# Gated adapter with layer norm on one core: the last batch's hidden stage made whole instead of by halves of its tokens

## The reference

```python
Wd = W_down[stream]; bd = b_down[stream]; Wu = W_up[stream]; bu = b_up[stream]
g = ln_w[stream]; b = ln_b[stream]
h = jnp.einsum('bsh,bhk->bsk', hidden_states, Wd) + bd[:, None, :]
h = jax.nn.gelu(h, approximate=False)
h = jnp.einsum('bsk,bkh->bsh', h, Wu) + bu[:, None, :]
h = hidden_states + h
mean = jnp.mean(h, axis=-1, keepdims=True)
var = jnp.mean(jnp.square(h - mean), axis=-1, keepdims=True)
h = (h - mean) * jax.lax.rsqrt(var + LN_EPS)
return h * g[:, None, :] + b[:, None, :]
```

## Time and profile before

| what | value |
|---|---|
| time, median of 3 runs | 72.03 us (71.99 to 72.11) |
| the profiled execution's own time | 72.03 us |
| its span, first to last instruction | 69.9 us |
| PE (TensorE matmul) busy | 57.6 us, 82% |
| DVE (VectorE) busy | 50.0 us, 72% |
| POOL (GpSimd) busy | 39.8 us, 57% |
| ACT (ScalarE) busy | 34.9 us, 50% |
| mean granted TensorE clock | 0.951 |

### The profile page before, as it was taken

One profiled execution on the slowest core, in us unless ns is written; L12 is line 12 of the kernel. 1 busy time (PEld: TensorE's weight loads), 2 busy tenths in 40 slices (PEclk: granted clock), 3 DMA queues, 4 the chain that ended last, 5 costly groups with the idle time before them and its releaser, 6 DMA issues. The chain is left out here.

```text
span 69.9 us, 947 instructions
## 1 busy us (share of the span) xinstructions
PE 57.6 (82%) x290; PEld 46.6 (67%) x290; DVE 50.0 (72%) x95; ACT 34.9 (50%) x51; POOL 39.8 (57%) x43
## 2 busy tenths in 40 slices
PE   1980199999499999999999999999999999994000
PEld 1960144489188888888887888888899989881000
DVE  0057005699929969883799989549999989999930
ACT  3300196898999800649998071999016504030000
POOL 4000060095199908999996599999929603038400
PEclk9999856999999999999999999999999999999955
DMA  0806999999999999999500006430000157210352
GB/s 0 265 35 161 344 246 401 416 414 413 415 412 414 413 411 417 397 413 415 206 16 0 0 5 260 197 143 0 0 9 0 61 239 300 86 65 5 148 203 100
DMA packets 4324, 14.75 MB, mean 211 GB/s; under 512 B 480, under 2 KB 480, under 8 KB 4320
## 3 DMA queue, kind: packets, MB, share of 16 engines
q1 hardware_dynamic: 4176, 14.17, 52.6%
q10 hardware_dynamic: 144, 0.52, 2.3%
HBM read 10.50 MB, written 4.19 MB: 210 GB/s over the span
## 5 line engine op out<-in xcount | busy, mean ns | idle before, releaser
L353 DVE BATCH_NORM_STATS2 stats<-y_ps 128x6 f32<-128x512 f32 x16 | 11.1, 694 | 4.2 <-PE y_ps L528 4.2
L522 PE MATMUL y_ps<-wu_hi,hid_hi 128*128 128x512 f32 x32 | 13.6, 424 | 0.0
L528 PE MATMUL y_ps<-wu_hi,hid_lo 128*128 128x512 f32 x32 | 12.8, 399 | 1.0 <-DVE hid_lo L342 1.0
L223 POOL TENSOR_TENSOR rstd<-var_eps,minus_half 128x2 f32<-128x2 f32 (+1 forms) x10 | 6.4, 641 | 12.2 <-DVE var_eps L361 12.2
L207 POOL TENSOR_TENSOR x_lo<-x_raw,x_hi 128x512 fp32r<-128x512 f32 x10 | 12.8, 1304 | 0.0
L524 PE MATMUL y_ps<-wu_lo,hid_hi 128*128 128x512 f32 x32 | 12.6, 393 | 0.0
L218 POOL TENSOR_TENSOR wu_lo<-w_raw,wu_hi 128x512 fp32r<-128x512 f32 x8 | 10.4, 1318 | 3.3 <-ACT wu_hi L274 3.3
L370 DVE SCALAR_TENSOR_TENSOR y_ps<-y_ps,mean_var,ln_gb 128x512 f32<-128x512 f32 x16 | 11.5, 749 | 0.0
L380 DVE SCALAR_TENSOR_TENSOR result<-y_ps,rstd,ln_gb 128x512 f32<-128x512 f32 x15 | 10.8, 744 | 0.3
L282 ACT ACTIVATE x_res<-x_raw,w_raw 128x512 f32<-128x512 f32 x16 | 10.3, 717 | 0.8 <-DMA x_raw<-x_cols 0.8
L334 DVE CAST x_hi<-x_raw 128x512 fp32r<-128x512 f32 x6 | 3.6, 596 | 9.5 <-DMA x_raw<-x_cols 9.5
(11 more groups left out here) (35 smaller groups left out, 84.9 us busy)
## 6 DMA issues: line engine op xcount, KB each, us to landing
x_raw<-x_cols SPq DMA_DIRECT2D x7, 512.0 KB, 11.5
out<-result SPq DMA_DIRECT2D x6, 512.0 KB, 2.6
w_raw<-weights SPq DMA_DIRECT2D x4, 516.0 KB, 10.9
w_raw<-weights SPq DMA_DIRECT2D x4, 512.0 KB, 11.6
ln_gb<-ln_rows SPq DMA_DIRECT2D x4, 512.0 KB, 14.8
out<-result SPq DMA_DIRECT2D x4, 256.0 KB, 2.4
x_raw<-x_cols ACTq DMA_DIRECT2D x1, 512.0 KB, 3.6
```

The lines of the kernel that those rows point to most:

```text
L353: nc.vector.bn_stats(stats[:, b % 2, t, :], y_ps[:, t, :]).then_inc(stats_done, 1)
L522: nc.tensor.matmul(y_ps[:, t, :], hid_hi[:, p, j, rows], wu_hi[:, p, j, :], start=False, stop=False, skip_group_check=True)
L528: last = nc.tensor.matmul(y_ps[:, t, :], hid_lo[:, p, j, rows], wu_hi[:, p, j, :], start=False, stop=(j == JT - 1), skip_group_check=True)
```

## The change

The last batch's down stage, gelu, subtraction and up stage are done as in the other batches. All helpers for halves go. The core of the diff:

```diff
@@ scalar @@
-                    gelu(b, 0)
-                    gelu(b, 1)
+                gelu(b, 0)
+                gelu(b, 1)
+                if b < LAST:
                     hi_x(b + 1, 1)
-            for half in range(2):
-                for j in range(JT):
-                    gelu_half(half, j)
@@ vector @@
-                if b + 1 < LAST:
-                    finish(b, 0)
-                    finish(b, 1)
-                    lo_hidden(b + 1, 0)
-                    finish(b, 2)
-                    finish(b, 3)
-                    lo_hidden(b + 1, 1)
-                else:
-                    finish(b, 0)
-                    lo_hidden_half(0, 0)
-                    finish(b, 1)
-                    lo_hidden_half(0, 1)
-                    finish(b, 2)
-                    lo_hidden_half(1, 0)
-                    finish(b, 3)
+                finish(b, 0)
+                finish(b, 1)
+                lo_hidden(b + 1, 0)
+                finish(b, 2)
+                finish(b, 3)
+                lo_hidden(b + 1, 1)
...
-                if t == 0:
-                    lo_hidden_half(1, 1)
@@ tensor: up @@
-                if b == LAST and t >= 2:
-                    n += JT
-                if t == 0 or (t == 2 and b == LAST):
+                if t == 0:
@@ tensor @@
-            for b in range(LAST):
+            for b in range(B):
...
-            down_half(0, 0)
-            down_half(0, 1)
-            down_half(1, 0)
-            place_residual(LAST, 0)
-            place_residual(LAST, 1)
-            up(LAST, 0, 0)
-            up(LAST, 0, 1)
-            down_half(1, 1)
-            up(LAST, 1, 0)
-            up(LAST, 1, 1)
-            for t in range(2, TT):
-                place_residual(LAST, t)
-                for j in range(JT):
-                    up(LAST, t, j)
```

More of the change, by code:

```diff
@@ L136, in conditional_adapter_kernel @@
         EARLY = KT + HALF
[L138 to L142, removed]
         SHARED_T = 1
@@ L291, in gelu @@
                                      bias=bias_down(b, j)).then_inc(hid_done, 1)
[L293 to L299, removed]
             act.dma_start(x_raw[:, 0, 0:HALF, :], x_cols[0, :, 0:HALF, :]).then_inc(x_in[0][0], DMA)
@@ L343, in lo_hidden @@
                                         ALU.subtract).then_inc(hid_lo_done, 1)
[L345 to L349, removed]
             def tile_stats(b, t):
@@ L480, in down @@
                 last.then_inc(hid_ps_done, 1)
[L482 to L500, removed]
             def place_residual(b, t):
```

## The result

The changed kernel took 73.3 us in the median of 4 runs (72.96 to 73.56), the kernel before 72.01 (71.98 to 72.11): ratio 1.0174, 95% interval 1.013 to 1.0218. It is slower by 1.3 us; the forecast was 73.44 with a range of 73.15 to 73.8. The profiled execution is the slowest of the four, 73.56 us with a span of 71.4. Three single runs further on (72.86 us of the kernel before, 73.94 and 72.93 of two of the experiments) lie over 1.5% above the fastest run of their kernel, and the ratios leave them out.

A forecast was written before the change was run, and what follows sets the result against it. The prediction took tile 0's arrival at VectorE plus a fixed VectorE chain as the bound. Its terms, 1.15 + 0.69 - 0.33 - 0.10 = +1.41 us on 72.03, gave 73.44 us, range 73.15 to 73.8.

The forecast's parts named there:

- What bounds the kernel: End of the last batch: the moment tile 0 reaches VectorE plus a fixed VectorE chain of 9.77 us before the change.
- Down stage, +1.15: TensorE, last batch: all the down stage precedes the residuals, 5.47 us instead of 4.32, so they begin 1.15 us later.
- Order of the up stage, +0.69: TensorE, last batch: tile 1's first group comes between tile 0's two groups, 2.72 us instead of 2.03, 0.69 us more.
- Gelu and subtraction hidden: Last batch: second half's hid_lo is ready at 58.08, wanted by the ninth product at 58.64, 0.56 us to spare.
- The chain, -0.33 and -0.10: VectorE after tile 0 arrives: fourth half subtraction (0.33 us) and wait for tile 2 (0.10) go, 9.77 becomes 9.34 us.
- The sum: VectorE's end in the last batch: 1.15 + 0.69 - 0.33 - 0.10 = +1.41 us, 68.42 against 67.01.
- The prediction's bounds: Whole time: 73.2 to 73.8 us from down stage, 0.10 wait, last store and 0.12 us run spread; widened to 73.15 below.
- the prediction's signs of being wrong: Last batch: tile 0's statistics before 58.8, a TensorE wait for hid_lo, or a chain under 9.2 or over 9.6 us.
- Saturated VectorE: Rival: VectorE's total work sets the end, so fewer, larger instructions save 0.53 us, time 71.50; chance 0.02.
- No change: Rival: the later delivery is taken up between tile 0 and the end, 1.41 us of slack, time about 72.0; chance 0.02.
- the third rival: Tail: tile 3's small variance instruction meets GpSimd work, or hid_lo comes over 0.56 us late; 0.53 us more, 73.97; chance 0.07.

The follow-up runs named there:

- the pair of delays: Changed kernel plus five unused matmuls of 512 columns, ahead of tile 2's residual in one run (73.4 us), ahead of tile 0's in the other (74.43 us).
- the fourth piece moved: Kernel before with the down stage's fourth piece ahead of the residuals and its subtraction behind batch 2's last finish; 72.81 us, ratio 1.0122.
- the two kernels shown above: Changed kernel with both groups of tile 0 first (72.83 us); kernel before with only the bottleneck's second half by halves of the tokens (72.21 us).
- tile 2 shared: The version with the subtraction moved, plus tile 2's last-batch finish on ScalarE and GpSimd and tile 3's store ahead of tile 2's; 71.89 us, ratio 0.9981.
- the version with the subtraction moved: Kernel before with the bottleneck's first half whole, second by token halves, its first half subtraction ahead of batch 2's fourth finish; ratios 0.9965 and 1.0022.

## Why the prediction was right

*What bounds the kernel.* Tile 0's arrival plus a fixed chain, and not TensorE's end nor VectorE's total: shown by the pair of delays (1.13 us cost 1.13 ahead of tile 0 and nothing ahead of tile 2), and by the fourth piece moved, where VectorE's work is the same and the end later.

*Down stage, +1.15.* Confirmed at 5.47 us against 4.32. It is the net of two things that the experiments part: the fourth piece ahead of tile 0 costs 1.42 us (8.21 - 6.79), wholes instead of halves give back 0.27 (8.89 - 8.62).

*Order of the up stage, +0.69.* Confirmed alone: 7.48 - 6.79 = 0.69. In the changed kernel it cannot be taken back in full, since tile 0 then runs into the second subtraction: 0.40 came of it.

*Gelu and subtraction hidden.* Ready at 57.51 + 0.69 = 58.20, used at 58.77: 0.57 us to spare, forecast 0.56.

*The chain, -0.33 and -0.10.* 9.33 to 9.34 us in every kernel with no subtraction in it, against 9.34 forecast. With the subtraction and without the wait for tile 2 it is 9.67.

*The sum.* +1.39 in the profile against +1.41. The median came to +1.29 against the kernel before's first runs, and to +1.58 when the changed kernel was run again. The two profiles put their own difference before the last batch; for the runs without a profile that is argued, not shown. The prediction's bounds held this spread too small: it took the first runs' 0.12 us for it, and it is over ten times that. That the median of four runs fell within 0.14 us of the forecast is in part luck; the terms were each measured. None of the prediction's signs of being wrong showed: the statistics began at 59.20, TensorE waited for no `hid_lo`, and the chain took 9.33 us.

*Rivals.* Saturated VectorE fell, though its 0.3 us of waiting after 50 us looked like saturation: an engine that hardly waits starts to wait once its next delivery comes later (1.91 us in three waits after the change). No change fell with the +1.39 us. Tile 3's L339 took 0.15 us as before and met no GpSimd work, so the third rival did not occur either.

## What to carry to other kernels

At the end of a pipeline, read which delivery starts the final chain, and count what stands in front of that delivery on the delivering engine: while the receiving engine waits there, work of another tile placed ahead costs its full length, even if the engine's total work shrinks. Whole instructions are cheaper per piece (here 12 ns for each matmul saved), but in the last stage the first piece's latency counts, not the sum. And compare versions from a fixed point in the trace when the start of the program varies: in the two kernels profiled twice the tail repeats to 0.01 us, where times spread by over 1 us.

## What was not expected of the hardware

A matmul that had waited for its operand took 0.50 us instead of 0.39 to 0.40 and held up the next by 0.11 us, in the two kernels shown above and in the one with tile 2 shared. A short stall so costs about 0.1 us more than the wait.

The batches repeat exactly (12.73 to 12.77 us from one down stage to the next), while the last batch's first matmul lies between 49.96 and 50.58 us over the profiles. The mean granted clock does not sort these: with 1.00 from the start to 15 us it began at 49.96 in one profile and at 50.55 in another, both of the version with the subtraction moved. What does was not tested.

The small L361 of batch 2 that took 0.70 us before, by the earlier trace rows, ended at 48.71, and GpSimd's subtractions at 48.68. In the kernel with tile 2 shared, GpSimd's ended later and L368, the same instruction there, took 1.10 us:

```profile
48.11 1.10 DVE L368 TENSOR_SCALAR var_eps<-mean_var 128x2 f32<-128x2 f32 x1
```

```profile
46.63 2.55 POOL L208 TENSOR_TENSOR x_lo<-x_raw,x_hi 128x512 fp32r<-128x512 f32 x2
```

Again it ended with them, 49.21 against 49.18. In all thirteen profiles it takes 0.69 to 1.10 us at this place and ends 0.02 to 0.03 us behind them; the second one of batch 2, with no GpSimd instruction beside it, takes 0.17 us. So it seems to be held until GpSimd's is done; no run took GpSimd's work away to show it. In the kernel with tile 2 shared the first subtraction of the last batch came 0.27 us later against the first matmul for it (4.86 instead of 4.59 us). TensorE's first product with that `hid_lo` waited 0.08 us and took 0.50, and tile 0 came 6.83 us after the first matmul instead of 6.65.
